# Both attention layers in pairs of heads: paired scores, two banks at a time, scores issued behind the projections

## The reference

```python
q, k, v = heads(layernorm(x) @ Wq), heads(ctx @ Wk), heads(ctx @ Wv)
s = q @ k.T * scale                  # 112 x 375 per head; layer 0 clamps it to +-10000
o = softmax(s) @ v
x = x + tanh(g_xattn) * (merge(o) @ Wo + bo)
x = x + tanh(g_ffn) * ffn(layernorm(x))
```

## Time and profile before

| | |
|---|---|
| time, median of 3 runs | 1280.2 us (1274.51 to 1282.06) |
| the profiled execution, its span | 1277.4 us (its own time isn't given apart) |
| busy: PE, DVE, ACT, POOL | 1066.5 (83%), 948.8 (74%), 567.6 (44%), 268.6 (21%) us |
| attention layer 0, first scores to last maxima | 47.9 to 287.2 us |
| attention layer 1, first maxima to last scores | 645.9 to 977.5 us |

### The profile page before, as it was taken

One profiled execution on the slowest core, in us unless ns is written; L12 is line 12 of the kernel. 1 busy time (PEld: TensorE's weight loads), 2 busy tenths in 40 slices (PEclk: granted clock), 3 DMA queues, 4 the chain that ended last, 5 costly groups with the idle time before them and its releaser, 6 DMA issues.

```text
span 1277.4 us, 23029 instructions
## 1 busy us (share of the span) xinstructions
PE 1066.5 (83%) x7860; PEld 746.0 (58%) x7860; DVE 948.8 (74%) x2024; ACT 567.6 (44%) x1276; POOL 268.6 (21%) x303
## 2 busy tenths in 40 slices
PE   0688888882979999854688988998897699999997
PEld 0577777771634555643367877777776455455553
DVE  5588888897398888697567777777776667776775
ACT  3366666672433343441455556555555233222220
POOL 1422222202245563001000000000000013433331
PEclk9899999995699999896799999999998699999999
DMA  5000000001112122320000000000000231112100
GB/s 190 1 2 2 1 0 0 0 1 66 64 48 84 58 96 67 110 71 28 6 1 2 2 2 1 1 0 1 1 1 1 100 129 64 64 64 72 70 1 29
DMA packets 9935, 47.82 MB, mean 37 GB/s; under 512 B 1513, under 2 KB 3313, under 8 KB 6930
## 3 DMA queue, kind: packets, MB, share of 16 engines
q1 hardware_dynamic: 9874, 47.03, 10.7%
HBM read 45.92 MB, written 1.11 MB: 37 GB/s over the span
## 4 chain that ended last, share of the span: by engine, by line
PE 33%; DVE 30%; issue 20%; ACT 9%; POOL 5%; DMA 2%; DVEq 1%; ACTq 0%; POOLq 0%
PE pb L1119 8%; PE pb L1134 7%; POOL qz L1227 5%; DVE ST L844 4%; DVE ST L855 3%; DVE nm L850 3%; PE pb L640 2%; PE pb L613 2%; PE pb L597 2%; DVE ST L847 2%; ACT ST L728 2%; PE pb L1424 2%; PE pb L576 1%; ACT V L711 1%; PE pb L570 1%
## 5 line engine op out<-in xcount | busy, mean ns | idle before, releaser
L1119 PE MATMUL pb<-xT,KT 128*128 128x448 f16 x1248 | 244.2, 354 | 2.7 <-DVE qz L1197 2.7
L1227 POOL TENSOR_TENSOR qz<-qz,Z 128x448 f32<-128x448 f32 x128 | 169.1, 1331 | 286.8 <-ACT qz L1166 197.5
L1119 PEld LDWEIGHTS pb<-xT,KT 128*128 128x128 f16 x1248 | 121.6, 98 | 119.6 <-DVE qz L1197 5.8
L613 PE MATMUL pb<-KT,qz 128*112 128x375 f16 (+1 forms) x768 | 171.8, 334 | 3.2 <-POOL qz L921 2.1
L640 PE MATMUL pb<-V,ST 125*112 125x32 f16 (+1 forms) x1536 | 127.0, 214 | 53.2 <-DVE ST L855 52.9
L1134 PE MATMUL pb<-V,KT 128*128 128x448 f16 x816 | 162.6, 357 | 8.9 <-DVE V L1206 8.9
L640 PEld LDWEIGHTS pb<-V,ST 125*112 125x112 f16 x1536 | 109.9, 133 | 71.3 <-DVE ST L855 47.2
L736 ACT ACTIVATE ST<-pb 125x336 f16<-125x336 f32 x256 | 113.6, 444 | 45.1 <-PE pb L623 42.5
L855 DVE SCALAR_TENSOR_TENSOR ST<-pb,ST 125x336 f16<-125x336 f32 x256 | 127.7, 499 | 6.0 <-ACT ST L736 5.4
L1134 PEld LDWEIGHTS pb<-V,KT 128*128 128x128 f16 x816 | 80.3, 99 | 86.3 <-DVE V L1206 10.5
L623 PE MATMUL pb<-identf,ST 112*125 112x112 f32 x768 | 125.8, 273 | 1.6 <-ACT ST L728 1.6
(11 more groups left out here) (196 smaller groups left out, 1594.0 us busy)
## 6 DMA issues: line engine op xcount, KB each, us to landing
ST<-in_moe SPq DMA_DIRECT2D x9, 1536.0 KB, 7.8
ST<-in_moe SPq DMA_DIRECT2D x8, 1024.0 KB, 6.8
Z<-wd_scratch SPq DMA_DIRECT2D x16, 448.0 KB, 4.4
ST<-in_ctxT SPq DMA_DIRECT2D x4, 750.0 KB, 4.9
ST<-in_gens SPq DMA_DIRECT2D x2, 768.0 KB, 4.7
ST<-in_lora SPq DMA_DIRECT2D x2, 624.0 KB, 8.7
ST<-in_w1q SPq DMA_DIRECT2D x1, 1024.0 KB
ST<-in_w1k SPq DMA_DIRECT2D x1, 1024.0 KB
```

Source lines behind the costliest of these rows:

```text
L613: mm = pe.matmul(SB_[st % 2][0:S, 0:L.keys], qz[:, bs % 2, qa, h, :], kT[bs % 2][qb][:, h // L.per_tile, 0:L.keys], start=(n == 0), stop=( ...
L1119: mm = pe.matmul(banks[m % len(banks)][:, 0:HT], MW[:, es % 2, qa, c:c + 128], xT[:, qb, k, half * HT:(half + 1) * HT], start=(i == 0), st ...
L1227: pool.tensor_tensor(tile, tile, wdB[:, es % 2, half * HT:(half + 1) * HT], ALU.mult)\
```

## The change

Heads go in pairs p = 0 to 7 through both layers.
- Layer 1 pairs heads 2p and 2p+1, which have rows 0 to 63 and 64 to 127 of one tile. Layer 0 pairs heads two apart (0 and 2, 4 and 6, 1 and 3, 5 and 7, then the same plus 8). The scores' products take only the rows of their head: 64 of 128 in layer 1, 32 in layer 0. In layer 0 a slice of 32 rows holds two heads, so the query is kept twice (`qv`), once with the odd heads' rows scaled by zero and once with the even ones' (`par`, two columns made once from `mask`); ScalarE and VectorE each do two instructions for a query unit instead of one. The masks of GpSimd go.
- The six products of a pair alternate between its heads, one in each of the two banks of `SP2`. Both banks now belong to one pair, so the next pair's scores wait for all of this pair's maxima (layer 0) or exponentials (layer 1), where a head's waited for the head two before.
- Layer 1's maximum is one reduction over both banks, layer 0's two with one clip of both. `turn` fills both banks of `TP2` with six transposes; `hi` and `lo` take both banks in one instruction each. `patches` take a pair.
- In step p TensorE issues transposes of pair p-1, weighing of p-2, the units of both heads' steps, and then the scores of pair p+1. `hi` and `lo` in step p are those of pair p-1. `normalise` stands at a lag of two pairs (`NORM_LAG`).

```diff
@@ -149,1 +154,1 @@
-        P_ = flat[0:S, 0:2 * KV].rearrange("p (a n) -> p a n", a=2)
+        P_ = flat[0:S, 0:4 * KV].rearrange("p (a j n) -> p a j n", a=2, j=2)
...
+        SC = flat[0:S, 4100:4100 + 4 * KV].rearrange("p (a j n) -> p a j n", a=2, j=2)
+        mask = sb("mask", [128, 8])
+        par = sb("par", [128, 2])
...
+        order = [0, 2, 4, 6, 1, 3, 5, 7]
+        self.order = list(range(H)) if index else order + [8 + h for h in order]
+        self.pairs = [self.order[2 * p:2 * p + 2] for p in range(NP)]
...
+        SP2 = ctx.enter_context(nc.psum_tensor("sp", [128, 2, 512], F32))
+        TP2 = ctx.enter_context(nc.psum_tensor("tp", [128, 2, 512], F32))
+        pb = [SP2[:, 0, :], SP2[:, 1, :], TP2[:, 0, :], TP2[:, 1, :]] + \
+             [ctx.enter_context(nc.psum_tensor(f"pb{i}", [128, 512], F32))[:, :] for i in range(4, 8)]
...
-                if st >= 2:
-
-                    pe.wait_ge(s["mx_done0"] if l == 0 else s["exp_done1"], i - 1)
+                if st >= 1:
+
+                    pe.wait_ge(s["mx_done0"] if l == 0 else s["exp_done1"], 2 * i)
                 for n, (qa, qb) in enumerate(PARTS):
-                    mm = pe.matmul(SB_[st % 2][0:S, 0:L.keys], qz[:, bs % 2, qa, h, :],
-                                   kT[bs % 2][qb][:, h // L.per_tile, 0:L.keys], start=(n == 0), stop=(n == 2))
+                    for j, h in enumerate(L.pairs[p]):
+                        if l == 0:
+                            t, r = h // 8, slice(32 * (h % 8 // 2), 32 * (h % 8 // 2) + 32)
+                            q = qv[r, bs % 2, h % 2, qa, t, :]
+                        else:
+                            t, r = h // 2, slice(64 * (h % 2), 64 * (h % 2) + 64)
+                            q = qz[r, bs % 2, qa, h, :]
+                        mm = pe.matmul(SB_[j][0:S, 0:L.keys], q, kT[bs % 2][qb][r, t, 0:L.keys],
+                                       start=(n == 0), stop=(n == 2))
...
@@ tensor, batch @@
-                for h in range(H):
-                    scores(bv, bs, h)
-                    if bs or h >= 2:
-                        turn(bv * H + h - 2, bs * H + h - 2)
...
+                for p in range(NP):
+                    if bs or p >= 1:
+                        turn(bv * NP + p - 1, bs * NP + p - 1)
+                    if p >= 2:
+                        weigh(bv, bs, p - 2)
+                    elif bs:
+                        weigh(bv - 1, bs - 1, NP + p - 2)
                     for hh, kind, u, n, ns, _ in todo:
-                        if hh == h:
+                        if hh // 2 == p:
                             d = 1 if kind == "front" else -1
                             unit(kind, u, n, ns, bv + d, bs + d, behind)
+                    if p < NP - 1:
+                        scores(bv, bs, p + 1)
+                    elif where != "last":
+                        scores(bv + 1, bs + 1, 0)
@@ scalar @@
-                act.activation(PT[:, st % 2, 0, :, :], TB_[st % 2][0:CHUNK, 0:NCH * S]
-                               .rearrange("p (c n) -> p c n", c=NCH), ACT.Copy).then_inc(s[f"hi_done{l}"], 1)
+                act.activation(PT[:, st % 2, :, 0, :], TP2[0:CHUNK, :, 0:NCH * S], ACT.Copy)\
+                   .then_inc(s[f"hi_done{l}"], 1)
...
+                for p in range(NP):
+                    if bs or p >= 1:
+                        hi(bv * NP + p - 1, bs * NP + p - 1)
+                    for j in range(2):
+                        exps(bv, bs, p, j)
+                        for hh, kind, u, n, ns, nh in todo:
+                            if hh == 2 * p + j:
...
@@ vector @@
+                    for j in range(2):
+                        dve.tensor_scalar(SC[:, st % 2, j, :], SB_[j][0:S, 0:L.keys], -CLAMP, CLAMP, ALU.max, ALU.min,
+                                          accum_out=nm[:, c + j:c + j + 1]).then_inc(s["mx_done0"], 1)
+                    dve.wait_ge(s["mx_done0"], 2 * i + 2)
+                    dve.tensor_scalar(SC[:, st % 2, :, :], SC[:, st % 2, :, :], CLAMP, None, ALU.min)\
                        .then_inc(s["clip_done0"], 1)
                     return
-                dve.tensor_reduce(nm[:, st % 4:st % 4 + 1], src, AX.X, ALU.max, negate=True)\
+                dve.tensor_reduce(nm[:, c:c + 2], SP2[0:S, :, 0:L.keys], AX.X, ALU.max, negate=True)\
                    .then_inc(s[f"mx_done{l}"], 1)
...
@@ gpsimd @@
-                            pool.tensor_tensor(qz[:, bs % 2, q, 8 * t:8 * t + 8, :],
-                                               bc(qu[:, bs % 2, q, t, :].unsqueeze(1), [128, 8, S]),
-                                               bc(mask[:, :].unsqueeze(2), [128, 8, S]), ALU.mult)\
-                                .then_inc(s["qz_done0"], 1)
...
-            attention_gpsimd(pool, layers[0])
```

More of the change, by code:

```diff
@@ L625, in turn, with weigh @@
+                if st >= 1:
+                    pe.wait_ge(s[f"lo_done{l}"], i)
+                for j in range(2):
+                    for c in range(NCH):
+                        mm = pe.transpose(TB_[j][0:CHUNK, c * S:(c + 1) * S],
+                                          P_[:, st % 2, j, c * CHUNK:(c + 1) * CHUNK], identf[0:S, 0:S])
                 mm.then_inc(s[f"t_mm{l}"], 1)
-            def weigh(bv, bs, h):
-                i, st = bv * H + h, bs * H + h
-                if h == 0:
+            def weigh(bv, bs, p):
+                i, st = bv * NP + p, bs * NP + p
+                if p == 0:
@@ L671, in attention_tensor @@
             batch("last", B - 1, B - 1)
[L672 to L675 removed]
+            turn(B * NP - 1, B * NP - 1)
+            weigh(B - 1, B - 1, NP - 2)
+            weigh(B - 1, B - 1, NP - 1)
             for _, kind, u, n, ns, _ in tail_units(L):
@@ L697, in unit @@
                 if u[0] == "q" and l == 0:
-                    act.activation(qu[:, bs % 2, 0, :, :], bank[:, 0:2 * S].rearrange("p (t n) -> p t n", t=2),
-                                   ACT.Copy, scale=QSCALE[0]).then_inc(g_hi, 1)
+                    for v in range(2):
+                        x = act.activation(qv[:, bs % 2, v, 0, :, :], bank[:, 0:2 * S].rearrange("p (t n) -> p t n", t=2),
+                                           ACT.Copy, scale=par[:, v:v + 1])
+                    x.then_inc(g_hi, 1)
                 elif u[0] == "q":
@@ L765, in attention_scalar @@
             batch("last", B - 1, B - 1)
-            for i in range(B * H - 2, B * H):
-                hi(i, i)
+            hi(B * NP - 1, B * NP - 1)
             for _, kind, u, n, ns, nh in tail_units(L):
@@ L879, in batch @@
                 todo = unit_numbers(L, where, bv, bs)
[L880 to L896 removed]
+                for p in range(NP):
+                    maxima(bv, bs, p)
+                    if bs or p >= 1:
+                        lo(bv * NP + p - 1, bs * NP + p - 1)
+                    for j in range(2):
+                        for hh, kind, u, n, ns, nh in todo:
+                            if hh == 2 * p + j:
+                                d = 1 if kind == "front" else -1
+                                unit(kind, u, n, ns, nh, bv + d, bs + d)
+                                if u[0] == "i":
+                                    ipa_rest(bv + d, bs + d)
+                        for g in range(L.groups) if j == 0 else ():
+                            at = (g + 1) * L.grouped // 2 - 1 + NORM_LAG
+                            if at == p:
+                                normalise(bv, bs, g)
+                            elif at == p + NP and bs:
+                                normalise(bv - 1, bs - 1, g)
             for _, kind, u, n, ns, nh in prologue_units(L):
@@ L907, in attention_vector @@
             batch("last", B - 1, B - 1)
-            for i in range(B * H - 2, B * H):
-                lo(i, i)
+            lo(B * NP - 1, B * NP - 1)
             normalise(B - 1, B - 1, L.groups - 1)
```

172 lines of the change are left out of this document (65 added, 107 removed).

## The result

The changed kernel takes 1345.9 us (median of four runs, 1339.0 to 1346.7) against 1279.6 (four runs, 1274.5 to 1282.1): ratio 1.051, 95% interval 1.048 to 1.054. It is **5% slower**. The forecast was 1261, with a range of 1243 to 1290; 1345.9 lies outside it. The profiled execution spans 1344.4 us where the one before spans 1277.4, +67.0.

What follows compares the result with a forecast made beforehand. It took layer 0 as bound by no single full engine, and layer 1 by TensorE in most heads and the VectorE-ScalarE round in some. Layer 0 -4 and layer 1 -15 made -19 us: 1261 us, range 1243 to 1290.

Steps and rivals of the forecast that it cites:

- rival 2: Layer 0: less TensorE work lets the clock fall to 1.2 GHz half the time, 25 us, total 1280 to 1286; chance 0.08.
- rival 1: Row groups don't overlap: each pair's scores take 0.42 us longer, 27 us in layer 1, total 1291; chance 0.2.
- the -4: Layer 0's forecast gain in us: seven batches -3.5, the first wait -2.1, the last batch +1.5.
- the first wait: Layer 0: the first batch stops waiting 2.08 us for GpSimd's masks, counted as -2.1.
- (d): Layer 0, pairs with units: rounds of 3.7 to 4.5 us, making a batch of eight pairs 30.1 against 30.6.
- (c): Layer 0, pairs without a unit: shorter lag makes ScalarE's loop 2.84 us per pair, against 2.54 now.
- (a): Layer 0: GpSimd's masks go, giving VectorE about 2.05 us per batch; the first batch stops waiting 2.08 us.
- step (h): Layer 1: pair by pair times with units, 41.9 us a batch against 44.37, a gain of 2.45.
- (e): Layer 1: a pair's six score products overlap in two row groups, taking 0.52 us instead of 0.94.
- (g): Layer 1: next pair's scores wait for both exponentials; a pair with two key units takes 4.02 us, TensorE waiting 0.5.
- The term: Layer 1's forecast gain: -15 us, from -17 over seven batches and +2 for the last.

Runs made afterwards that it cites:

- e5: Changed kernel with both heads of a layer 0 pair on rows 0 to 31, so their scores cannot overlap: 1395.8 us, ratio 1.092.
- e10: e3 with layer 0's scores, in single heads and the old order with masks, cut to rows 0 to 31: 1421.5 us, ratio 1.111.
- e1: Changed kernel with layer 0's paired scores on all 128 rows, one head behind the other, attention computed wrongly: 1263.75 us, ratio 0.990.
- e3: Only layer 1 in pairs as in the change, layer 0 as in the kernel before: 1270.6 us, ratio 0.994.
- e9: e3 with both heads of a layer 1 pair on rows 0 to 63, so their scores cannot overlap: 1297.2 us, ratio 1.015.
- e6: Changed kernel plus four idle 128-row products before each pair's transposes in layer 0, bank wait moved first in both layers: 1277.1 us, ratio 0.999.
- e2: Changed kernel with 64 rows a head in layer 0's scores instead of 32, still side by side: 1300.4 us, ratio 1.019.
- e8: e3 with 32 rows a head instead of 64 in layer 1's scores: 1272.8 us, ratio 0.995.
- f2: Changed kernel plus two idle 128-row products before each pair's transposes, in layer 0's branch alone: 1365.7 us, ratio 1.068.
- f3: Changed kernel plus three idle 128-row products before each pair's transposes, in layer 0's branch alone: 1382.1, 1304.8, 1304.5 and 1269.5 us, no ratio.
- e7: Changed kernel plus six idle 128-row products before each pair's transposes in layer 0, bank wait moved first in both layers: 1275.3 us, ratio 0.998.

## Why the prediction was wrong

**The step that failed is rival 2, the clock**, and with it every duration of layer 0. The sum of the forecast has no term for the clock. Rival 2, where it stood, was priced at 25 us and a chance of 0.08, with the reason that "a low clock would make TensorE the busy one and so raise it again". TensorE did become the busy one, 98 to 100% of layer 0, and the clock stayed at 0.50 (after, e5, e10). The rival rested on stalls of TensorE and on a loss of 3.4 us of work; what lowers the clock is the rows of the scores, which e10 shows in the order of before. Nothing in the prediction asks what shape the remaining products have.

The size could have been estimated. The trace before has a stretch at the low level, from which the clock comes back by itself (three score products at the low level, then three at the full level):

```profile
57.35 1.14 PE L613 MATMUL pb<-KT,qz 128*112 128x375 f16 x3
...
61.96 0.64 PE L613 MATMUL pb<-KT,qz 128*112 128x375 f16 x3
```

That is 1.8 times as long. Rows of the change give 1.60 against 0.91 for six transposes and 1.26 against 0.75 for twelve weighing products (the latter in e1 at 183.13), some 1.7. TensorE's 27.01 us of a batch less 3.4 are 23.6, and 1.7 times that makes an estimate of 40 us a batch (measured 40.8), where VectorE's pace was forecast at 30.1: 8 x 10 = 80 us. Measured, change against e1, 82.8. A rival "full layer at the low clock" would have stood near 1340. (The range was also drawn 1 us short of rival 1's 1291.)

The Trainium skill, page "TensorE: Matmul & The Clock Gate", Part 1, ties the clock to how busy TensorE has been of late. The rows here differ: 50.0 of 50 us busy at 0.50 (e5, e10) and 40.3 of 50 at 1.00 (e3). The measurement decides.

**Layer 0 with the clock held** (e1) is 8.8 us shorter than before, where the same stretch was forecast at -2 (the -4 less the first wait of 2.1, which lies ahead of it). 2.7 of that goes with the clock: e3's layer 0 is the kernel before at 1.00 where it had 0.90 to 0.96, and takes 245.0 instead of 247.7. The other 6.1 are the pairs. The steps were right in kind; (d) was some 0.9 us a batch too long. In e1 the eight pairs of a batch take 4.44 + 4.17 + 4.09 + 3.57 + 3.75 + 3.58 + 2.39 + 3.22 = 29.2 us from maxima to maxima, where (d) had 30.1: the pair with a normalisation and a key takes 4.17 and not 4.5, the one with the query 4.44 and not 4.1, the one with output and value 3.75 and not 4.3, and the two without a unit take the 5.6 of (c). Seven batches take 202.8 us against 216.0, -13.2 where -3.5 was forecast; the last batch with the output behind it takes 4.2 more where 1.5 was set, so the two errors partly cancel. In (a), 2.05 us does not follow from "the same rate", which would give 1.11 / 1.47 x 6.92 = 5.2; the clips that run beside masks were 14.9 us longer in all of layer 0 before, 1.9 a batch, so the amount was right.

**Layer 1** went as written. Distances between a pair's scores and the next, from 789.63 on in the trace after, against step (h):

| pair | 2 values | 3 values | queries | behind | transposes + keys | 2 keys | 2 keys | short keys, value, output | sum |
|---|---|---|---|---|---|---|---|---|---|
| forecast | 4.45 | 5.7 | 5.15 | 4.87 | 5.5 | 4.02 | 4.34 | 7.85 | 41.9 |
| measured | 4.51 | 5.90 | 5.23 | 4.85 | 5.65 | 4.10 | 4.33 | 8.0 | 42.6 |

Overlap (e) and wait (g) are shown by the trace and by e9. The term was -15 and is -9.4: the first seven batches give -13.0 (306.8 to 293.8) where -17 was forecast, and the last one with the output behind it +3.6 where +2 was set. Rival 1 did not occur. Its price, 27 us, was met by e9 in the sum but not in its parts (0.35 a pair in seven batches, 1.0 in the last), so that is in part luck. Nothing was set for the stretches outside the layers, which take 4.2 us more in the change and 4.1 in e3 (351.1 - 348.7 and 287.0 - 285.3). The first of them, between the layers, takes 344.9 in e5, which has the code of the change there, so it also varies by itself; why was not looked into.

**The best kernel that computes all of the reference** is e3, 1270.6 us, 0.6% under the kernel before. e6 shows layer 0 in pairs with the clock held at 240.8, but at 1277.1 it is no gain. Layer 0 in pairs with scores on all 128 rows and masks, which e1 comes near to, was not built.

## What to carry to other kernels

Cutting products to few rows may save time on TensorE and still cost more than it saves, as it did here in layer 0. Before choosing row groups, count what is left on TensorE and price the whole stretch at the low clock, not a part of it. Row groups paid where more work on all rows stood around them (layer 1, e3). The check is one look at the clock of the windows. Where the clock is low although TensorE is full, look at the shape of its products, not at its waits.

## What was not expected of the hardware

- In the same order and with the same columns, layer 0 ran at a granted clock of 1.00 with scores on 128 rows and 0.50 on 32 (e3, e10); in pairs 1.00, 0.71 and 0.50 on 128, 64 and 32 rows (e1, e2, after).
- In layer 1, 32 rows left it at 1.00 (e8). Which property of the other products makes the difference stays open.
- Four added products on 128 rows, of 0.84 us in all per pair, brought layer 0 from 0.50 to 1.00 (e6); two did not (f2); with three, executions of one kernel lay between 1269.5 and 1382.1 us (f3).
- Six products in two row groups took 0.68 us at full clock and 1.19 at half; on the same rows 1.15 and 2.12 (e9, e5).
- e6 had 55 packets in its instruction queue against 37 in e7, and waits of TensorE without a releaser at the turn of layer 1's loop, where two of its batches were 11 us longer in sum; the cause was only argued.
- With scores on 128 rows the clock came back from the low level by itself, in the kernel before at about 61 us; with 32 rows and TensorE 98 to 100% busy it did not in some 300 us (after).
